# A vision-tower layer on one core: the feed-forward product of two sub-tiles as seven block products

## The reference

```python
A = -exp(inv_A_real) + 1j * A_imag; dtA = A * exp(log_dt)[:, None]
Cc = B * C * (exp(dtA) - 1) / A                 # C is x, read as complex
h = 2 * einsum('chn,hnl->chl', Cc, exp(dtA[:, :, None] * arange(1024))).real
h = h + layernorm(h) @ attn_weight.T + attn_bias
n = layernorm(h)
gates = softmax(n @ Wr.T)                       # 4 experts
lora = einsum('bse,bseo->bso', 2 * gates, (n @ A.T per expert) @ Bm per expert)   # rank 8
out = h + n @ W.T + b + lora
```

## Time and profile before

| | us |
|---|---|
| median of 3 runs (lowest, highest) | 809.19 (808.93, 809.88) |
| span of the profiled execution, first to last instruction | 805.8 |
| PE busy | 769.3 |
| DVE busy | 622.0 |
| ACT busy | 527.3 |
| POOL busy | 5.5 |

### The profile page before, as it was taken

One profiled execution on the slowest core, in us unless ns is written; L12 is line 12 of the kernel. 1 busy time (PEld: TensorE's weight loads), 2 busy tenths in 40 slices (PEclk: granted clock), 3 DMA queues, 4 the chain that ended last, 5 costly groups with the idle time before them and its releaser, 6 DMA issues.

```text
span 805.8 us, 14896 instructions
## 1 busy us (share of the span) xinstructions
PE 769.3 (95%) x5334; PEld 377.3 (47%) x5334; DVE 622.0 (77%) x1229; ACT 527.3 (65%) x881; POOL 5.5 (1%) x22
## 2 busy tenths in 40 slices
PE   2759899999999999999999999999999999999997
PEld 1634344444444444444444444444444444444443
DVE  7899978777777787787878877777887778777532
ACT  6778876667676766766677576667766676765210
POOL 2000000000000000000000000000000000000000
PEclk9988999999999999999999999999999999999999
DMA  7869942434343333334333342434324333433323
GB/s 287 295 123 173 153 81 55 98 67 86 80 95 62 70 80 78 78 75 99 80 67 71 67 98 55 99 80 83 70 57 95 70 83 80 93 61 71 57 53 81
DMA packets 196109, 74.65 MB, mean 93 GB/s; under 512 B 184496, under 2 KB 189488, under 8 KB 195960
## 3 DMA queue, kind: packets, MB, share of 16 engines
q1 hardware_dynamic: 195992, 74.26, 42.8%
q10 hardware_dynamic: 96, 0.13, 0.0%
HBM read 14.06 MB, written 16.78 MB: 38 GB/s over the span
## 4 chain that ended last, share of the span: by engine, by line
PE 86%; DVE 4%; SPq 4%; ACT 2%; DMA 2%; issue 1%; ACTq 0%
PE ps_g L531 39%; PE ps_g L591 37%; PE ps_a L522 5%; PE ps_g L597 2%; PE ps_g L697 1%; PE ps_p L579 1%; SPq L378 1%; SPq L361 1%; DMA x<-in_L_attn_weight 1%; DVE wa_lo L1238 1%; DMA x<-x_tok 1%; PE ps_p L581 1%; ACT phase L736 0%; SPq L437 0%; DMA x<-stage 0%
## 5 line engine op out<-in xcount | busy, mean ns | idle before, releaser
L531 PE MATMUL ps_g<-wa_hi,x 128*128 128x512 f16 x1024 | 271.6, 381 | 8.3 <-DMA wa_lo<-h_tok 7.2
L591 PE MATMUL ps_g<-wf_hi,x 128*128 128x512 f16 x992 | 261.0, 379 | 0.2 <-DMA wf_lo<-stage 0.2
L531 PEld LDWEIGHTS ps_g<-wa_hi,x 128*128 128x128 f16 x1024 | 98.0, 98 | 130.6 <-issue 16.2
L531 PE MATMUL ps_g<-wa_lo,x 128*128 128x512 f16 x512 | 154.5, 381 | 0.0
L591 PE MATMUL ps_g<-wf_lo,x 128*128 128x512 f16 x496 | 148.8, 379 | 0.0
L591 PEld LDWEIGHTS ps_g<-wf_hi,x 128*128 128x128 f16 x992 | 94.9, 98 | 110.7 <-DMA wf_lo<-stage 0.7
L1198 DVE SCALAR_TENSOR_TENSOR result<-ps_g,unscale,h_tok 128x1024 f32<-128x1024 f32 x31 | 39.8, 1284 | 88.2 <-PE ps_g L597 88.2
L768 ACT ACTIVATE junk<-ps_a,stat 128x1024 bf16<-128x1024 f32 x32 | 35.2, 1101 | 68.8 <-DVE stat L1105 68.8
L531 PEld LDWEIGHTS ps_g<-wa_lo,x 128*128 128x128 f16 x512 | 50.2, 98 | 60.6 <-issue 0.8
L591 PEld LDWEIGHTS ps_g<-wf_lo,x 128*128 128x128 f16 x496 | 48.5, 98 | 58.3
L774 ACT ACTIVATE junk<-h_tok,stat 128x1024 bf16<-128x1024 f32 x32 | 36.8, 1149 | 52.2 <-DVE stat L1145 52.2
(11 more groups left out here) (214 smaller groups left out, 881.4 us busy)
## 6 DMA issues: line engine op xcount, KB each, us to landing
out<-result SPq DMA_DIRECT2D x124, 128.0 KB, 2.2
stage<-in_L_ffn_W SPq DMA_DIRECT2D x8, 512.0 KB, 14.1
x_raw<-in_x SPq DMA_DIRECT2D x38, 64.0 KB
wf_hi<-in_x SPq DMA_DIRECT2D x1, 2048.0 KB, 9.1
h_tok<-in_L_attn_weight SPq DMA_DIRECT2D x2, 512.0 KB, 4.1
x<-in_L_attn_weight SPq DMA_DIRECT2D x2, 512.0 KB, 8.1
result<-in_L_attn_weight SPq DMA_DIRECT2D x2, 512.0 KB, 9.5
x<-x_tok SPq DMA_TRANSPOSE x64, 3.2
```

The costliest lines, as they stand in the source:

```text
L531: mm = pe.matmul(ps[:, o, :], x1_part(part, ps is ps_g2)[:, k, :], ws[:, k, o * HALF:(o + 1) * HALF], start=k == 0 and part == 0 and ws is ...
L591: pe.matmul(ps_g2[:, o, :], xs[:, k, :], ws[:, k, o * HALF:(o + 1) * HALF], start=k == 0 and xs is x2_hi and ws is wf_hi, stop=False)
```

## The change

From tile 2 on (FIRST = 2) the feed-forward product of a tile is made for both sub-tiles together. With A the 256 x 1024 tokens, cut in four blocks (sub-tile by half of the input columns), and W cut in four 512 x 512 blocks, seven block products replace eight (Winograd's form of Strassen's scheme). Each is 4 blocks x 3 parts = 12 matmuls of 128x512 into one bank.

- Tokens: A11, A12 and A22 are blocks of the normalised sub-tiles, and S1, S2, S4, S3 are sums and differences, which POOL makes in one chain behind normalise_2(t, 1). ACT splits each of them (high_form, 128x512), DVE makes the low part (low_form), and SP transposes each with one DMA, in the order S1, S2, S4, S3, A22. S1 and S3 share a slot in form_tok: the high part of S3 waits for the transpose of S1.
- Weights: T1 to T4 are sums of weight blocks. In tiles 1 and 2 four portions are loaded again (load_again), summed by POOL, split by ACT and DVE (high_sums, low_sums) and transposed (turn_sums). Product 5 of tile 2 waits for all 16 transposes, and so does POOL's first addition.
- The banks: bank_a, bank_b (ps_g2) and bank_c (ps_x). Eight takes of 128x512 add a bank to the residual in place of two finishes of 128x1024. Products 1, 6, 7 build up in bank_a, and each is taken before the next is added.
- Both sub-tiles share one projection (project_pair), one gate and one transpose of the low-rank vectors. The second row of blocks uses S1 and A22 with a difference of the projection weights.
- From sub-tile (3, 0) on, ACT writes y from ps_a (Identity with scale and bias), and DVE makes only the one-column shift for it.
- h2_tok and result become `residual`, two buffers by the parity of the tile. The scratch for dynamic DMAs is 1024 bytes.

PE's order for a tile is now as follows, where before two steps of s4, attn, project, ffn stood. Tile 2's feed-forward product is in pair_step(3), so tiles 1 and 2 end with s4(3, 0), attn(2, 1), and s4(3, 1) directly behind.

```diff
+            def second_products(t):
+                tau = t - FIRST
+                pe.wait_ge(s_pair_t, 16 * tau + 16)
+                add_lora(bank_b, 0, 0).then_inc(s_product, 1)
+                pe.wait_ge(s_form_t[S4], 16 * tau + 16)
+                pe.wait_ge(s_taken, EACH * tau + 2)
+                add_form(bank_c, S4, plain(1, 1), False)
+                add_lora(bank_c, 0, 1).then_inc(s_product, 1)
+                pe.wait_ge(s_form_t[S3], 16 * tau + 16)
+                pe.wait_ge(s_taken, EACH * tau + 3)
+                add_form(bank_a, S3, added(T3), False).then_inc(s_product, 1)
+                pe.wait_ge(s_form_t[A22], 16 * tau + 16)
+                pe.wait_ge(s_taken, EACH * tau + 4)
+                add_form(bank_b, A22, added(T4), True)
+                add_lora(bank_b, 1, 0).then_inc(s_product, 1)
...
+            def pair_step(t, ended=True):
+                s4(t, 1)
+                if ended:
+                    last_lora(t - 2)
+                attn(t, 0)
+                project_pair(t - 1)
+                product_1(t - 1)
+                product_2(t - 1)
+                product_5(t - 1)
+                product_6(t - 1)          # bank_a: waits for take_p1
+                if not isinstance(t, int) or t < TILES - 1:
+                    s4(t + 1, 0)
+                attn(t, 1)
+                second_products(t - 1)
```

DVE's order:

```diff
+            def pair_step(t, p, ended=True, following=True):
+                    keep_h(t, 1)
+                    end_22(t - 2, p)
+                        make_m(t + 1, 0)
+                    normalise_1(t, 1)
+                        round_turns(t + 1, 0)
+                    low_1(t, 1)
+                        low_m(t + 1, 0)
...
+                keep_h2(t, 0, p)
+                    make_u(t + 1, 0)
+                pair_gate_begin(t - 1)
+                normalise_2(t, 0, p)
+                take_p1(t - 1, 1 - p)
+                pair_gate_end(t - 1)
+                    low_u(t + 1, 0)
+                low_first(t)
+                take_p5(t - 1, 1 - p)
+                take_p6(t - 1, 1 - p)
+                    next_h(t + 1, 0, t, 1, True)   # keep_h, make_m, normalise_1, round_turns, low_1, low_m
+                keep_h2(t, 1, p)
+                    make_u(t + 1, 1)
+                end_11(t - 1, 1 - p)
+                normalise_2(t, 1, p)
+                end_12(t - 1, 1 - p)
+                low_form(t, A22, 2)
+                low_form(t, S1, 3)
+                take_p7(t - 1, 1 - p)
+                low_form(t, S2, 4)
+                    low_u(t + 1, 1)
+                low_form(t, S4, 5)
+                low_form(t, S3, 6)
+                end_21(t - 1, 1 - p)
```

ACT's second half of a tile, and POOL's list:

```diff
+                square_2(t, 1, p)
+                rstd_guess(t, 1, stat_2, s_ssq2, s_log2, s_y2)
+                high_form(t, A22, 0)
+                high_form(t, S1, 1)
+                high_form(t, S2, 2)
+                    high_u(t + 1, 1)
+                high_form(t, S4, 3)
+                high_form(t, S3, 4)       # waits for the transpose of S1
                 split_x(t + 2)
                 waves_ahead(t + 2, 0)
                 join_x(t + 2)
...
+            def add_forms(t):
+                pool.wait_ge(s_xn2, 2 * t + 2)
+                pool.tensor_tensor(form_sum[:, :], xn_b[:, 0:HALF], xn_b[:, HALF:L], ALU.add).then_inc(s_form, 1)
+                pool.tensor_tensor(xn_b[:, 0:HALF], form_sum[:, :], xn[:, 0:HALF], ALU.subtract).then_inc(s_form, 1)
+                pool.tensor_tensor(xn[:, HALF:L], xn[:, HALF:L], xn_b[:, 0:HALF], ALU.subtract).then_inc(s_form, 1)
+                pool.tensor_tensor(xn[:, 0:HALF], xn_b[:, HALF:L], xn_b[:, 0:HALF], ALU.subtract).then_inc(s_form, 1)
```

More of the change, by code:

```diff
@@ L61 @@
 LORA_POWER = 2.0 ** 16
+FIRST = 2
+ACT_FROM = 6
+A11, A12, S1, S2, S4, S3, A22 = range(7)
+FORMS = 7
+EACH = 8
+LOWERED = 6
+T1, T3, T2, T4 = range(4)
 def at_least(engine, semaphore, value):
@@ L677, in step, with add_form, add_lora @@
                 ffn_end(*b)
+            def add_form(bank, f, weights, start):
+                for k in range(KB // 2):
+                    for part, w in ((0, 0), (0, 1), (1, 0)):
+                        mm = pe.matmul(bank, form_part(f, part)[:, k, :], weights(w, k),
+                                       start=start and k == 0 and part == 0 and w == 0,
+                                       stop=k == KB // 2 - 1 and part == 1, skip_group_check=True)
+                return mm
+            def add_lora(bank, i, o):
+                return pe.matmul(bank, lora_t_pair[0:KL, i, :], lora_rows(o), start=False, stop=True,
+                                 skip_group_check=True)
@@ L1443, in step, with next_h @@
                 keep_h(*n)
+                make_m(t + 1, i)
+                normalise_1(*n)
+                round_turns(t + 1, i)
+                low_1(*n)
+                low_m(t + 1, i)
+                keep_h2(t, i, t % 2)
+                make_u(t + 1, i)
+                gate_begin(*b)
+                normalise_2(t, i, t % 2)
+                gate_end(*b)
+                low_u(t + 1, i)
+                low_2(t, i)
+            def next_h(T, i, t, k, following):
+                keep_h(T, i)
@@ new lines, in _ @@
+            step(1, 0)
+            low_sums(0)
+            difference_of_lora_a()
+            step(1, 1)
+            low_sums(1)
+            finish(1, 0)
+            next_h(2, 1, 2, 0, True)
+            keep_h2(2, 0, 0)
+            make_u(3, 0)
+            gate_begin(1, 1)
+            normalise_2(2, 0, 0)
+            gate_end(1, 1)
+            low_u(3, 0)
+            low_first(2)
+            low_sums(2)
+            finish(1, 1)
+            next_h(3, 0, 2, 1, True)
+            keep_h2(2, 1, 0)
@@ new lines, in _ @@
+            make_u(3, 1)
+            low_sums(3)
+            normalise_2(2, 1, 0)
+            low_form(2, A22, 2)
+            low_form(2, S1, 3)
+            low_form(2, S2, 4)
+            low_u(3, 1)
+            low_form(2, S4, 5)
+            low_form(2, S3, 6)
+            pair_step(3, 1, ended=False)
+            with dve.Fori(2, TILES // 2 - 1) as two:
+                pair_step(2 * two, 0)
+                pair_step(2 * two + 1, 1)
+            pair_step(TILES - 2, 0)
+            t = TILES - 1
@@ L1480 @@
+            pair_step(t, 1, following=False)
+            end_22(t - 1, 0)
+            take_p1(t, 1)
+            pair_gate_begin(t)
+            pair_gate_end(t)
+            take_p5(t, 1)
+            take_p6(t, 1)
+            end_11(t, 1)
+            end_12(t, 1)
+            take_p7(t, 1)
+            end_21(t, 1)
+            end_22(t, 1)
 _INS = ["x", "L0_tok_log_dt", "L0_tok_B", "L0_tok_inv_A_real", "L0_tok_A_imag", "L0_attn_weight",
```

571 lines of the change are left out of this document (457 added, 114 removed).

## The result

The changed kernel takes 901.93 us (median of 4 runs, 901.22 to 902.87) against 809.06 for the kernel before on the same chip, a ratio of 1.116 with an interval of 1.114 to 1.117. That is 11.6% slower. The sign was forecast; the size was not: 838 us was said, and 870 was the end of the range.

A forecast was written before the change was run, and what follows sets the result against it. PE was taken as the bound (100 of 100 us busy); 43.7 us of PE work plus waits 2.0 and 1.7 gave 47.4 a tile. Start 196.3, twelve tiles to 763.2, end 68.8, then 2.8 and 3.4: 838 us, range 812 to 870.

The forecast's parts named there:

- The saving: A tile's feed-forward product goes from 96 matmuls to 84, saving 2.59 us a tile, 36.3 us over 14 tiles.
- Rival 4: The edit does not save what it says because single-bank products are slower; excluded by 5.19 us for 24 matmuls.
- The section from keep_h2(t,1) to the end of low_u: Chain behind attn(t,1): normalising to xn_b 5.2 us, POOL's S1 and S2 2.2, then split, u and low_u; 10.2 us.
- wait A: PE idle before s4(t,1), waiting for low_u(t+1,1): 2.0 us a tile, 1.4 if POOL cost nothing.
- rival 1: GpSimd and DVE hold each other up beside the four sums: wait A 4.3, tile 49.7, total 868 us; chance 0.22.
- Wait B: PE idle before product 6, delayed through S1's transpose, S3 and join_x: 1.7 us a tile, bounds 0 to 3.5.
- rival 3: The waits feed each other once DVE's 0.8 us slack before attn(t,1) is gone: period 48.5, 851 us; chance 0.10.
- The clock: Granted clock 0.50 after PE's long wait at the fill: 2.3 us added once, nothing for waits of 2 us.
- The set-up: Block sums of the weights, before attn(2,1) ends, fit in DVE's waits of 2.98 and cost 1 us.
- The fill: PE stands 14.2 us between attn(2,1) and s4(3,1); bounds 10.3, or 20 if the reloads are late.
- The end: From s4(15,1) to DVE's end, 68.8 us, including a 4.8 us wait for end_21(14).
- Rival 2: PE stays the bound: 794 us, or 818 with wait B alone gone; chance 0.09 with a gain, 0.02 no change.

The follow-up runs named there:

- the first of the last two kernels: The reordered kernel with take_p7 ahead of S1's low split on VectorE and attn(3,0) ahead of s4(3,1) on TensorE; 832.09 us, ratio 1.031.
- the reordered kernel: The changed kernel with u first in both halves, x transposed early, the set-up reordered, and take_p1 and low_u ahead of the gate; 830.25 us, ratio 1.027.

## Why the prediction was wrong

1. *The saving (2.59 us a tile, 84 matmuls at 0.216).* Right: in the chain of waits a product of 12 matmuls into one bank takes 2.59 us at full clock, and two of them 5.19. Rival 4 was rightly excluded.
2. *The section from keep_h2(t,1) to the end of low_u (10.2 us in wait A).* This is the step of the loop that failed. It took 12.8 us, with 0.1 to 0.2 of it before s4 begins. The two sums that it holds took 1.27 + 1.60 and gaps for my 2.2 (+0.7), low_u began 0.5 later because the split of S2 was stretched to 1.1, and low_u took 2.28 for 1.2 (+1.1). All but some 0.4 us are rival 1; the 0.4 is that an addition alone takes 1.27 for my 1.05. Rival 1 was given 0.22 and a period of 49.7; its mechanism was right, and I had let the silence of POOL in the loop of before count as "neither for nor against" instead of as a price not known.
3. *Wait B (from s4(t,1) to product 6, 22.4 + 0.1 us).* 366.70 to 389.81 is 23.1: right within 0.7. That wait B came out at 0.6 and not 1.7 is luck in the parts: PE arrived 1.8 us later than I had it, 1.3 of it by the half clock of s4. In sum, 12.8 for 10.4, 23.1 for 22.4 and 14.7 for 14.5 are 50.6 for 47.3.
4. *That A and B are two waits.* I added them to PE's 43.7, and said in rival 3 alone that they might feed each other. They are the ends of two rings of nearly one length, 50.0 and 50.6. So the sum over PE happened to be near, while the reading "take away 2 us of wait A and win 2" was false. Wait A was taken away whole with u first (+13 us), by 3.1 us with the small sums (-20 us, since the sums stand in the x ring too) and filled with matmuls (+6 us).
5. *The clock.* I wrote "none shows it for waits of 2 us, where I add nothing". After 4.4 us it was 0.50, and s4 took 2.75. In the tiles in which the x ring is the longer one it is hidden; in the four in which the half clock lasts on, it sets the period. In the kernel with u first, where it falls on product 6, it costs 2 us a tile. And it did fall behind waits of 2 us, in other kernels, as the last section shows.
6. *The set-up (1 us).* The other step that failed. I had costed DVE's 2.9 us in DVE's waits and not asked what the added DMAs are queued ahead of on SP. attn(2,1) ended 13.6 us late (213.68 - 20.30 = 193.4 for 179.8), and 11.27 of that is one wait. Four transposes and two reloads stand ahead of the x halves, and everything up to the low-rank vector waits for these. Mended, it gave 10.3.
7. *The fill (14.2).* It was 20.3, at my upper bound "20 if the reloads are late": the last reload is issued at 188.26 behind transposes and lands at 194.3, and four POOL additions of 1.3 to 2.1 us follow one another. low_u(3,1) stood behind S2 and so behind all of this; with u first the same wait is 13.0 us. The 2.3 us for the clock came later than I had put them, in s4(3,1) itself (2.75 for 1.49) and behind it.
8. *The end (68.8).* 74.1: half clock on s4(15,1) and on the first matmuls behind it (0.50 until 827.5, 2.6 us together) and on two products (6.69 for 24 matmuls where 5.19 was the price), and 1.1 for take_p7. The wait for end_21, forecast 4.8, was 4.21. The rest of the 5.3 us, under 1, was not traced.
9. *Rival 2* had a gain only if A and B together stay under 1.3 us. In the best order that was run, PE's waits are 1.9, and the ends cost 24 where I had 15 to 20; it is out even so.

In short, the loop's step that failed is the section behind keep_h2(t,1), priced at 10.4 us without the hold-ups and measured at 12.8, together with a clock that I put at nothing; and outside the loop it is the 1 us for the set-up, which was 14.6 (193.4 for 178.8). That most of the loss can be undone by order alone, 72 of 93 us, the forecast did not see.

## What to carry to other kernels

When an engine that was silent is given work on SBUF, price each instruction of its neighbour that reads two SBUF tensors at its row and what is left of the instruction that it may come behind (0.4 to 1.1 us here), until a run shows otherwise. Put what the longest ring needs first: what came first kept its row. Close each wait to a ring, all the way round to the same instruction one tile on, through SP's queue and the DMAs too; where two rings are within a microsecond of each other, no edit to one of them alone will show a gain of more than that, and a failed one proves little about its cause. A scheme that saves matmuls on the bound engine pays its depth twice, at the start and at the end: count the products left behind the last token product before the savings of the loop.

## What the runs showed that I had not expected

- The granted clock after a wait of PE is not settled by the wait alone. It was 0.50 after 4.4 us. A product of 12 matmuls behind 5.8 us took 4.72 us, and one behind 1.99 us took 4.25, while products behind 2.15 and 3.21 us took 2.76, full clock. In one and the same run (the first of the last two kernels) a wait of 1.99 us stood before 4.25, 4.45 and 2.76. The Trainium skill (TensorE: Matmul & The Clock Gate, "What's actually happening") has the array come back at 1.2 GHz after it was idle; here that holds for every wait of 4 us and more that was looked at, and in some cases for 2 to 3.3.
- DVE and POOL take turns, and who comes first decides who pays. Behind an addition, low_u went from 1.22 to 2.28 us and a cast of 128x64 from 0.20 to 1.06. With low_u ahead of the addition, as in the reordered kernel, low_u keeps its row and the addition goes from 1.27 to 2.08:

```profile
428.07 1.22 DVE L1449 TENSOR_TENSOR u_split<-turn,u_split 128x1024 f16<-128x1024 f32 x1
```

```profile
428.34 2.08 POOL L1400 TENSOR_TENSOR form_sum<-xn_b 128x512 f32<-128x512 f32 x1 [38.85 <-DVE xn_b L1568]
```

  low_u ends at 429.2, and 1.27 us behind that is 430.4, the end of the addition. DVE's takes from PSUM (0.74) did not change beside additions.
- An addition of 128x512 takes 1.27 us on POOL alone. The line through its two smaller sizes gave 1.02; the estimate from the Trainium skill (GPSIMD Engine Reference, 3.1), 1.24, was the better one.
